# Attention on one core: shift rows copied in a row beside two V products, and the weight's passes ahead of the P sums

## The reference

```python
b, s1, _ = x.shape
q = _ln((x @ Wq + bq).reshape(b, s1, H, HD), qn_w, qn_b)
kv = jnp.concatenate([y_main @ Wk + bk, y_main @ Wv + bv], axis=-1)
# k, v of y_main; k_dca, v_dca of y_dca, the last 16 rows
ctx = _attn(qT, k.transpose(0, 2, 1, 3), v.transpose(0, 2, 1, 3))
ctx_dca = _attn(qT, k_dca.transpose(0, 2, 1, 3), v_dca.transpose(0, 2, 1, 3))
ctx = ctx + DCA_WEIGHT * ctx_dca
return ctx @ Wo + bo
...
x = x + _L0_xattn_ref(_layernorm(x, axis=-1), ctx_1024, ...)
x = x + _L0_ffn_ref(_layernorm(x, axis=-1), ...)
```

## Time and profile before

| | |
|---|---|
| median of 3 runs | 1087.1 us (1086.47 to 1091.04) |
| the profiled execution | 1091.38 us, its span 1089.7 us |
| busy in the span: TensorE | 937.6 us (86%) |
| VectorE | 647.4 us (59%) |
| ScalarE | 463.3 us (43%) |
| GpSimd | 616.2 us (57%) |
| attention stage | from 173.3 to 453.2 us of the span |

### The profile page before, as it was taken

How to read it: one execution, slowest core, us unless ns; L and a number is a source line. 1 busy time by engine, 2 the same in 40 slices (tenths; PEclk the granted TensorE clock), 3 DMA queues, 4 the chain that set the end, 5 groups by cost and what they waited for, 6 DMA issues and landing times. The chain is left out here.

```text
span 1089.7 us, 17150 instructions
## 1 busy us (share of the span) xinstructions
PE 937.6 (86%) x5077; PEld 403.4 (37%) x5078; DVE 647.4 (59%) x1025; ACT 463.3 (43%) x846; POOL 616.2 (57%) x566
## 2 busy tenths in 40 slices
PE   3788984898898898799984699999999999998498
PEld 1444441111121121266531245445445444553133
DVE  8777777787787884377652244444455554442078
ACT  2465565777777776333520022223223223223040
POOL 6465554466766764432064289898899993004700
PEclk9999995999999999899995899999999999999689
DMA  7135435344444321143345555555556553347703
GB/s 260 44 108 154 142 105 173 120 149 165 164 155 164 104 74 60 40 136 117 116 166 184 181 174 191 168 185 178 185 192 192 186 177 125 109 171 269 218 20 136
DMA packets 104521, 162.31 MB, mean 149 GB/s; under 512 B 10904, under 2 KB 53912, under 8 KB 104080
## 3 DMA queue, kind: packets, MB, share of 16 engines
q1 hardware_dynamic: 91520, 116.45, 32.7%
q0 software_dynamic: 12896, 45.10, 12.3%
q10 hardware_dynamic: 48, 0.05, 0.0%
HBM read 108.08 MB, written 53.48 MB: 148 GB/s over the span
## 5 line engine op out<-in xcount | busy, mean ns | idle before, releaser
L1048 DVE TENSOR_REDUCE nm<-a_psS 128x4 bf16<-128x1984 f32 x62 | 138.3, 2230 | 55.5 <-PE a_psS L1106 53.6
L1005 ACT ACTIVATE p_t<-a_psT 128x512 f32<-128x512 f32 x256 | 138.9, 595 | 67.5 <-PE a_psT L1121 65.8
L956 POOL TENSOR_TENSOR p_sum<-p_t,p_t 128x512 f32<-128x512 f32 x64 | 81.5, 1273 | 94.6 <-ACT p_t L1005 93.6
L1874 PE MATMUL e_psU<-w_exp,e_xT 128*128 x456 | 107.4, 386 | 7.7 <-issue 4.0
L1874 PE MATMUL e_psY<-w_exp,e_gT 128*128 x456 | 110.7, 379 | 0.9 <-ACT e_y L1815 0.9
L1874 PE MATMUL e_psG<-w_exp,e_uT 128*128 x456 | 104.9, 380 | 2.5 <-DVE e_uT L1829 2.5
L205 POOL TENSOR_TENSOR w_exp<-e_raw,w_exp 128x1024 f32 (+1 forms) x42 | 90.6, 2157 | 6.0 <-POOL e_raw L202 4.5
L1121 PE MATMUL a_psT<-q_stk,k_stk 98*128 98x512 f16 x256 | 85.6, 399 | 4.0 <-ACT p_t L1005 1.5
L197 POOL TENSOR_TENSOR w_exp<-e_raw,ws_tile 128x1024 f32 (+1 forms) x42 | 80.3, 1911 | 6.5 <-DMA e_raw<-in_L_ffn_Wup_dram 5.6
L1801 ACT ACTIVATE e_gT<-e_psGT 128x512 f16<-128x512 f32 x38 | 22.7, 597 | 123.4 <-PE e_psGT L1864 123.4
L1822 ACT ACTIVATE e_g<-e_g 128x512 f32<-128x512 f32 x38 | 23.9, 630 | 106.8 <-DVE e_g L1832 106.8
(11 more groups left out here) (326 smaller groups left out, 1816.0 us busy)
## 6 DMA issues: line engine op xcount, KB each, us to landing
xs_dram<-zero SPq DMA_DIRECT2D x38, 256.0 KB, 5.3
e_x<-xs_dram SPq DMA_DIRECT2D x38, 256.0 KB, 4.0
bias<-in_L_ffn_bup_dram SPq DMA_DIRECT2D x38, 256.0 KB, 3.8
bias<-in_L_ffn_bgate_dram SPq DMA_DIRECT2D x38, 256.0 KB, 3.7
ys_dram<-e_y SPq DMA_DIRECT2D x38, 256.0 KB, 3.8
q_dram<-q_st SPq DMA_DIRECT2D x24, 256.0 KB, 3.0
k_dram<-k_st SPq DMA_DIRECT2D x24, 256.0 KB, 3.7
q_stk<-q_dram SPq DMA_DIRECT2D x64, 96.0 KB
```

The costliest lines, as they stand in the source:

```text
L956: pool.tensor_tensor(p_sum[:, w % SUMS, :], probs(w, 0), probs(w, 1), ALU.add).then_inc(s["sum_1"], 1)
L1005: act.activation(probs(w, k), psT[:, k % 2], ACT.Exp, scale=SCALE / (QS * QS)).then_inc(s["exp"], 1)
L1048: dve.tensor_reduce(nm[:, i, :, 0:1].rearrange("p h o -> p (h o)"), psS[:, :, 0:NMAIN], AX.X, ALU.max, negate=True)
L1874: ins = pe.matmul(dst[:, :], stationary, moving, start=(k == 0 and chunks[0] == 0), stop=(k == len(terms) - 1 and chunks[-1] == KD - 1))
```

## The change

TensorE's order of a period is written anew. `max_rows` and `scores(p, 0)` open the period instead of closing the one before; the last pair of the group in its exponentials crosses the period's border and follows them, and then come V products 0 and 1 with no pair between. The P sums' denominators stand behind `scores(p, 1)`, and `last_sums` behind a pair of its own. ScalarE copies the four shift rows in a row at the period's start, then takes the pair left over and the weight's cast, then the rest. GpSimd runs both weight passes and issues the next load ahead of the period's four P sums, where they stood at the third and fourth. VectorE's `inverses` stand behind `maxima(p, 3)`.

```diff
@@ GpSimd
+                    if n is not None and i == 0:
+                        low(n, 1)
+                        low(n, 2)
+                        if n + 1 < len(early):
+                            pool.wait_ge(g_["split_done"], n + 2)
+                            load(n + 1)
                     if scored(p - 1):
                         p_sums(G * (p - 1) + i)
...
-                    if n is not None and i >= 2:
-                        low(n, i - 1)
-                    if n is not None and i == 3 and n + 1 < len(early):
-                        pool.wait_ge(g_["split_done"], n + 2)
-                        load(n + 1)
@@ ScalarE
+                if scored(p - 1):
+                    for h in range(G):
+                        max_row(G * (p - 1) + h)
+                pair(p - 2, TB - 1, 1)
+                if n is not None:
...
+                    g_["scale_half"](act, raw[:, :, :], raw_ld, n + 1, k, half, m, n, 0)
                 for i in range(TB):
...
+                    pair(p - 1, i, 0)
+                    if i == 0 and scored(p - 3):
                         hi_part(p - 3)
+                    if i < TB - 1:
+                        pair(p - 1, i, 1)
@@ VectorE
                 if scored(p):
                     maxima(p, 3)
-                if scored(gr):
-                    scaled_dca(gr)
-                    main_inverse(gr)
-                    scaled_main(gr)
+                if scored(old):
+                    inverses(old)
+                    scaled_dca(old)
+                    main_inverse(old)
+                    scaled_main(old)
@@ TensorE
+                new, now, old = p, p - 1, p - 2
+                if scored(now):
+                    max_rows(now)
+                if scored(new) and new:
+                    scores(new, 0)
+                turned_pair(old, TB - 1, 1)
+                if scored(old):
+                    values(old, 0)
+                    values(old, 1)
+                if scored(new) and new:
+                    scores(new, 1)
+                if scored(old):
+                    sums(old)
+                turned_pair(now, 0, 0)
+                if scored(old):
+                    third_sums(old)
+                if scored(new):
+                    scores(new, 2)
+                turned_pair(now, 0, 1)
+                if scored(old):
+                    last_sums(old)
+                turned_pair(now, 1, 0)
+                if scored(old):
+                    values(old, 2)
+                if scored(new):
+                    scores(new, 3)
+                turned_pair(now, 1, 1)
+                if scored(old):
+                    dca(old)
+                turned_pair(now, 2, 0)
+                if scored(old):
+                    values(old, 3)
+                turned_pair(now, 2, 1)
+                turned_pair(now, 3, 0)
```

More of the change, by code:

```diff
@@ L1014, in hi_part, with pair @@
                 act.activation(oT_all[:, b, c, 0, :], r_main[:, gr % 2], ACT.Copy).then_inc(s["o_hi"], 1)
+            def pair(gr, i, half):
+                if scored(gr):
+                    exps(G * gr + i, 2 * half)
+                    exps(G * gr + i, 2 * half + 1)
             for p in range(PERIODS):
                 n = early_of(p)
-                for i in range(TB):
-                    for half in range(2):
-                        if scored(p - 1):
-                            exps(G * (p - 1) + i, 2 * half)
-                            exps(G * (p - 1) + i, 2 * half + 1)
-                        if i == 0 and scored(p - 1):
-                            max_row(G * (p - 1) + 2 + half)
-                        if i == TB - 1 and scored(p):
-                            max_row(G * p + half)
-                    if i == 1 and scored(p - 3):
-                        hi_part(p - 3)
-                    if n is not None and i == 2:
-                        m, k, half = early[n]
-                        if n == 0:
-                            for q in g_["qk_stored"][0] + g_["qk_stored"][1]:
-                                act.wait_ge(q, 3 * 16 * NT // PAIR // 2)
-                        g_["scale_half"](act, raw[:, :, :], raw_ld, n + 1, k, half, m, n, 0)
+                if scored(p - 1):
[3 more added lines that the diff above has]
+                if n is not None:
+                    m, k, half = early[n]
+                    if n == 0:
+                        for q in g_["qk_stored"][0] + g_["qk_stored"][1]:
+                            act.wait_ge(q, 3 * 16 * NT // PAIR // 2)
+                    g_["scale_half"](act, raw[:, :, :], raw_ld, n + 1, k, half, m, n, 0)
+                for i in range(TB):
+                    pair(p - 1, i, 0)
+                    if i == 0 and scored(p - 3):
+                        hi_part(p - 3)
+                    if i < TB - 1:
+                        pair(p - 1, i, 1)
         @block.vector
@@ L1079, in _ @@
             for p in range(PERIODS):
-                gr = p - 2
+                old = p - 2
                 if scored(p):
@@ L1170, in _, with turned_pair @@
-            for p in range(PERIODS):
-                for h in range(2 * TB):
-                    if h == 1 and scored(p) and p:
-                        scores(p, 1)
-                    if h == 2 * TB - 1 and scored(p):
-                        max_rows(p)
-                    if h == 2 * TB - 1 and scored(p + 1):
-                        scores(p + 1, 0)
-                    if scored(p - 2):
-                        chunk(p - 2, h)
-                    if scored(p - 1):
-                        scores_t(G * (p - 1) + h // 2, 2 * (h % 2))
-                        scores_t(G * (p - 1) + h // 2, 2 * (h % 2) + 1)
-                    if h == 2 and scored(p):
-                        scores(p, 2)
-                    if h == 2 and scored(p - 2):
-                        third_sums(p - 2)
-                    if h == 4 and scored(p):
-                        scores(p, 3)
+            def turned_pair(gr, i, half):
+                if scored(gr):
+                    scores_t(G * gr + i, 2 * half)
+                    scores_t(G * gr + i, 2 * half + 1)
```

20 lines of the change are left out of this document (2 added, 18 removed).

## The result

The changed kernel took 1075.2 us in the median (1073.1 to 1078.1), the kernel before 1089.0 on the same chip (1086.5 to 1091.0). The ratio is 0.988, with a 95% interval of 0.9865 to 0.9896: 13.1 us faster (11.3 to 14.7), where 24.0 were forecast (1063.1 us in the median). The sign was right and the size was not.

What follows compares the result with a forecast made beforehand. No engine is full; the order in which engines wait for each other sets attention's period. Gains of 22.5 and 3.3 less 1.8 lost make 24.0 us, from the median 1087.1 to 1063.1 us; range 1056 to 1075.5.

Steps and rivals of the forecast that it cites:

- The removed wait: TensorE ahead of the P sums' matmuls: the 1.57 us wait for the last shift row goes; matmuls start at 3.49.
- P = 14.7: Attention period for one group of four heads: 14.7 us in place of 16.43, between 14.4 and 15.5.
- The middle term: The 13 attention periods from group 2 to group 15: 22.5 us gained, between 26.4 and 12.1.
- SP's queue keeps its order: SyncE's queue in attention: order unchanged, and loads of q and k for a row have most of a period.
- The start: First turned groups, partly at the slow clock, four pairs behind scores 3 instead of two: 1.8 us lost, bounds 0 and 5.
- The end: From group 15's turned maxima to attention's last instruction: 3.3 us gained, bounds 0 and 4.
- A: Rival: ScalarE's block sets the period at 15.5 us, pair 0b waiting for its end; 1073.5 us, chance 0.15.
- B: Rival: GpSimd's queue replaces the removed wait, or the weight's load is late and takes ScalarE along; 1087 us, chance 0.06.
- C: Rival: TensorE's clock does not come up at the start, so slower; four such periods give 1111 us; chance 0.06.
- D: Rival: denominators held by the last P sum rather than the copies, at the same time; chance 0.06 together with B.
- GpSimd's cover: GpSimd's P sum 3 ends at P + 2.0, TensorE wants it at P + 3.5: 1.5 us of cover.
- VectorE's 0.15 us: VectorE's next reduction 0 may start at P + 0.6, its scores give 0.76: 0.15 us short of being the bound.

Runs made afterwards that it cites:

- woven start: Early spread kernel with the first turned group's period written in the old weave of pairs and scores; ratio 0.9788 to the kernel before.
- spread kernel: Changed kernel with no zero store for the first head of each group, so three heads in four issue one; ratio 0.9813 to the kernel before.
- first try at the start: Early spread kernel with pair 0a put back ahead of scores 1 in the first turned period alone; ratio 0.9798 to the kernel before.
- the experiment: Early spread kernel with three idle multiplications on GpSimd ahead of P sum 3, 2.49 us put in; periods 0.99 us longer, ratio 0.9921.
- light weight: Changed kernel with the 11 weight loads behind the first cut from 512 KB to 32 KB, output wrong; ratio 0.9749 to the kernel before.
- early spread: Changed kernel with zero stores for three heads in four, begun one group earlier; ratio 0.9785 to the kernel before.
- control: Kernel before with zero stores for three heads in four, begun one group earlier; ratio 1.0004, all 13 periods 16.43 us.

## Why the prediction was wrong, step by step
- **The removed wait.** Right. The 1.57 us for the shift row are gone, the P sums' matmuls stand at 3.51 (forecast 3.49), and the one wait left in an undisturbed period is that for the exponentials ahead of pair 3a. (A slip that nothing hangs on: 2.5 us of waits less 1.57 leave 0.9 in the old period, not 1.1.)
- **P = 14.7.** Right: 14.64 in ten of 13 periods of the kernel after, and in all 13 where no load is late. The middle term was 22.5; without late loads it is 13 x 1.79 = 23.3.
- **The step that failed** is the one sentence on SyncE: "SP's queue keeps its order, and its loads of q and k for a row have most of a period." It priced late loads of q and k at nothing. The lead was right for the old order (12.6 us of 16.43 for k_hi). In the new one it shrank to between 6.1 and 8.7, against up to 8.1 to landing, as the queue's issues got longer and it fell behind. The forecast moved the weight's load and shortened the period by a ninth, and did not raise the traffic per us for it. The cost was 7.7 us. In the profiled executions the 24.0 became 13.2 of span so: 0.8 more by the period, 7.7 less by late loads, 1.9 less at the end, 1.8 and 0.2 less outside the stage.
- **Which row would have told.** None by itself. The forecast left the DMA share of 0.47 in the earlier trace rows unused, and that is a mean. In the kernel before, stretches of four us already show 0.76 to 0.81 at the place of the weight's load, and 0.21 to 0.35 behind it:

```profile
264.00:268.00 4.00, 2.43 (x20) 0.53 (x22) 1.32 (x3) 2.42 (x6) 3.29 (x3) 1.00 0.78 264
268.00:272.00 4.00, 4.00 (x32) 0.76 (x24) 3.93 (x5) 2.37 (x5) 1.27 (x1) 1.00 0.24 89
```

  The kernel after has peaks of much the same height (0.72 over 280 to 284 us, 0.83 over 297.0 to 301.2), so a peak is no sign of late loads either. What could have warned is SyncE's own rows in the kernel before: an issue of q_hi, 0.42 us in the median, took 1.65 at 279.00, so issues could get longer.
- **The start.** Right in size: 1.8 lost, forecast 1.8, though one execution differs from another by up to 1.5 us here (37.0 to 38.5 us from the first scores to group 2's turn in the new order, 36.2 to 36.9 in the old). The woven start takes 2.3 us out of its own period, so the order of that one period is the cause.
- **The end.** Forecast 3.3, measured 1.4: group 15's turn to the last instruction took 28.6 where 26.7 were forecast. The V products ran slower there, with a granted clock of 0.53, than in the spread kernel, whose end took 26.9. Late loads are not the cause: the end took 28.6 in the first try at the start too, which had none, and 26.9 with the zero stores on ScalarE's queue, which had five. So the forecast's step was right to 0.2 us, and what lets the clock fall in two of nine traces stays open. After first, then the spread kernel:

```profile
426.26 3.52 PE L1133 MATMUL a_psO<-p_t,v_all 128*32 128x512 f32 x16
```

```profile
419.27 1.92 PE L1133 MATMUL a_psO<-p_t,v_all 128*32 128x512 f32 x16
```
- **The stage before it** began 1.8 us later in this execution. The forecast could not know that.
- **Rivals.** A's 1073.5 is near the measured time, and A is not what happened: no period was 15.5, ScalarE's block never held pair 0b. That 1075.2 lies inside the stated range, by 0.3 us under its top of 1075.5, is luck: the top was A's. B named a late load, but the weight's, through the cast, and ScalarE never waited for that one: it was issued 9.7 us ahead of the cast or more, and landed in 5.3 to 6.8 in the median, so that at least 2.9 us of the forecast's 3.9 were there. The loads that were late were k's. C's fear of the clock showed only in small, 3.0 us behind the waits in the middle. D did not happen: no wait for the P sums. GpSimd's cover was 1.5 us by the experiment. VectorE's 0.15 us was not measured; the trace has its first reduction directly behind the scaling, and no period longer for it.

With every load on time the change is worth about the 24 us that were forecast. The kernel with VectorE's part undone and the early spread, whose 13 periods are all 14.64, took 1065.4 us beside 1089.8 of the kernel before: 24.4 us, and the control shows that the spread alone brings nothing. Its stage takes 256.9 us to the next stage's first matmul, and the light weight's 257.1, where the kernel before has 281.3 and the kernel after 266.0.

## What to carry to other kernels
When a period gets shorter, everything that is carried per period gets denser: add up its bytes. A load's cover is the time from its issue to its use less its landing time under the traffic of the new order. Here the landing of k_hi went from 5.0 to 6.6 us, and the larger part was lost ahead of that: its issue came 4 to 6.5 us nearer to its use. So follow a load's lead over many periods; a queue that falls behind by half a us per period, as in the spread kernel, shows nothing in the first few. Background transfers that nobody waits for are the ones to thin out first.

## What the runs showed that was not expected
- The time of a DMA's issue on SyncE is no constant. A zero store of 256 KB took 0.46 us to issue in the median in the kernel before and with the light weight, 1.5 in the kernel after, and 0.34 from ScalarE's queue at the same pace. A load of 96 KB took 0.69 to 3.7.
- Two halves of a change may each cost 7% alone and save 1.2% together: GpSimd's order and ScalarE's place of the cast are one loop.
- A wait of TensorE of 0.67 us cost 2.2 and one of 0.85 cost 2.5, with a granted clock of 0.54 and 0.52 behind them. In other periods waits of 0.41, 0.77 and 0.95 cost 0.1 more than themselves at most. What decides it, no run shows.
